# Flamingo block on one core: routing spread over ScalarE and GpSimd, and the turn of the maxima moved ahead of a score group

## The chip, the cores and the metric

One NeuronCore of a Trainium2 chip runs the whole kernel. The metric is device time in microseconds (us) of one launch. TensorE multiplies matrices, VectorE, ScalarE and GpSimd (POOL in the profile) work element by element, and SyncE only issues transfers; the engines run their own instruction lists side by side and meet at semaphores.

## What is computed

The input is 8 batches of 256 tokens of width 128, with 64 context rows per batch. First attention, then a mixture of experts, each added to its input through a gate:

```
x = x + tanh(g_xattn) * attention(layernorm(x), ctx)     # 16 heads of 8, keys = 64 ctx rows + 256 tokens, causal
x = x + tanh(g_ffn)   * experts(layernorm(x))

# experts: T = 2048 tokens, E = 8 experts, top 2 of each token, H = 512
logits = xt @ Wg + bg
top_v, top_i = top_k(logits, 2)
label = one_hot(top_i).sum(1)
seq = cumsum(label, 0) * label            # running place of each token in each expert
valid = seq <= capacity                   # capacity = 320; later tokens are dropped
h = silu(disp @ W1) * (disp @ W2);  out = h @ W3
y = sum over the two choices of softmax(top_v) * out[place]
```

## The kernel before

**Stages.** Up to about 34 us all queries, keys and values are made and stacked. Then a loop of ticks handles 16 units (a unit is half the heads, four pairs, of one batch); two units make a batch. Behind it (from about 223 us) the experts run one after the other: transfers bring each expert's 320 rows, TensorE and ScalarE and VectorE compute, and GpSimd adds the answers into the output with indirect transfers, three for each expert, one expert after the other.

**The order in the loop** is written out by hand: each tick has 16 slots (`SL`), and each step of a unit or batch has a place `AT_...` counted from that unit's own tick. Every engine walks through the same ticks and slots and issues its own steps in them, so the order on an engine is that of the slots, and within a slot that of its code (on VectorE the maxima come first). Nothing but semaphores ties an engine's slot to another's. For batches `b >= LATE` (the last two) some steps have places of their own (`LATE_...`). A step of a batch is counted from its second unit.

**One unit.** In tick U-2 TensorE makes the scores of four pairs p (`scores`, slots 0, 4, 8, 12) and VectorE takes their maxima (`maxima`, L835 and L836, slots 2, 6, 10, 14). In tick U-1 TensorE turns the maxima into a row (`maxima_t`, slot 4), ScalarE copies it (L689, slot 5), and SyncE's queue moves it beside the queries. In tick U the transposed scores are made (`scores_t`, L1100), together with the scores of unit U+2, ScalarE takes exponentials (L696), and GpSimd masks them (L577, L580). In tick U+1 come the products with the values (`values`, L1120, slots 5, 7, 9, 11, 13) and ScalarE's copy of them (L707, slot 15). In tick U+2 they are turned (`turn_values`, L1153), inverted and normalised (L841, L851).

**One batch** then goes on: attention turned (L1161), projected (L1170), added to x (L867, `x1_done`), statistics, rstd on GpSimd (L588), normalised tokens (`tokens_out`, L881), tokens turned (L1179), copied by ScalarE (L717, and L718 for the second copy of the row), logits (L1185), then routing: `top_two` on VectorE in eight steps (top values, indices, one-hot, labels, running count), `positions` on TensorE (running place by products with a triangle and with ones), `destinations` in five steps (weights, place, overflow, row number), and `send_rows`, four indirect transfers by GpSimd (L598) into a DRAM table `slots_dram`, cleared before in four transfers (L570). A row is 128 token values, the token number, and the weight.

**Shared memory.** The eight PSUM banks are shared by time: bank 6 holds the value products and the turned maxima, bank 7 the turned values, the logits, the positions and, in its other half, the projected tokens. Many waits of TensorE guard these: `values` waits for ScalarE's copy of the row (`mrow_done`), `turn_tokens` for the normalised attention of the next unit (`att_done`), `turn_values` for the positions to have been read, and `positions` for `x1_done` of the next batch when `b < LATE`. `keep_active` issues filler products (L1058) on TensorE where it would have little to do.

## Time and profile before

| | |
|---|---|
| three runs | 308.89, 305.91, 308.52 us; median 308.52 |
| the profiled execution | 304.91 us, of which 303.1 us is the span of the trace |
| mean granted TensorE clock | 0.905 of 2.4 GHz |
| busy: TensorE, VectorE, GpSimd, ScalarE | 238.4, 174.1, 152.9, 132.0 us |
| chain that ended last, by engine | TensorE 34%, VectorE 14%, issue 14%, transfers 13%, GpSimd 13%, ScalarE 5% |
| loop of ticks | from about 34 to 200 us |
| expert stage | from about 223 us to the end |

The columns of a timeline row are start and duration in us, the engine, the line of the kernel, the instruction, the tile written and the tiles read, shapes, and how many were merged; in brackets stands how long the engine sat idle before and what released it. The profile was taken of one execution, so its durations add up to that one.

### The profile page before, as it was taken

To read this page: it belongs to the slowest core of one execution; us is meant where nothing else is said; L and a number is where in the kernel's file an instruction comes from. 1 tells how busy PE (TensorE), PEld (TensorE's weight loads), DVE (VectorE), ACT (ScalarE), POOL (GpSimd) and SP (SyncE) were. 2 spreads that over 40 slices of the span, in tenths; PEclk is the share of its full clock that TensorE was granted. 3 is DMA by queue.
4 is the path that set the end of the run, shared out by engine and by line. 5 is a ranking of instruction groups with operands and counts; after the bars stand their busy time and mean duration, and the time that the engine had idled before them with its cause. 6 is when DMAs were issued, how large, how long until landed. Compare 5 with 4: busy or idle time off the path is not lost.

```text
span 303.1 us, 6031 instructions
## 1 busy us (share of the span) xinstructions
PE 238.4 (79%) x2179; PEld 140.7 (46%) x2179; DVE 174.1 (57%) x532; ACT 132.0 (44%) x294; POOL 152.9 (50%) x213
## 2 busy tenths in 40 slices
PE   1767784888988777897997789885979999999800
PEld 0555322355554444454554444342346666666600
DVE  6479691758889899877758963544102333333400
ACT  6256501757665566655546666312013333333200
POOL 3699820445352763817417548355500555655661
PEclk9999966979999999977569999997889999999985
DMA  7131365464533226561010001001054455553220
GB/s 199 38 84 47 67 118 85 76 119 99 118 57 58 54 51 94 106 190 43 16 37 13 16 18 40 0 16 43 4 122 125 118 120 125 126 127 57 22 22 5
DMA packets 28764, 21.79 MB, mean 72 GB/s; under 512 B 4105, under 2 KB 26051, under 8 KB 28736
## 3 DMA queue, kind: packets, MB, share of 16 engines
q1 hardware_dynamic: 21632, 15.74, 22.7%
q0 software_dynamic: 4608, 4.16, 7.9%
q10 hardware_dynamic: 2496, 1.52, 2.5%
q8 instruction: 17, 0.28, 0.4%
q14 instruction: 11, 0.09, 0.1%
HBM read 9.27 MB, written 5.82 MB: 50 GB/s over the span
## 4 chain that ended last, share of the span: by engine, by line
PE 34%; DVE 14%; issue 14%; DMA 13%; POOL 13%; ACT 5%; ACTq 2%; POOLq 1%; SPq 1%; another core or an unknown queue 0%; DVEq 0%
PE PS L1120 11%; DMA out<-kst 7%; PE PS L1100 6%; POOL out L633 5%; DMA qst<-mrow 4%; DVE rows L881 2%; PE PS L1083 2%; DVE mxb L836 2%; DVE mxb L835 2%; PE PS L1058 2%; PE PS L1170 2%; ACT pt L696 2%; POOL slots L598 2%; PE PS L1274 1%; PE PS L1276 1%
## 5 line engine op out<-in xcount | busy, mean ns | idle before, releaser
L696 ACT ACTIVATE pt<-PS 128x512 f32<-128x512 f32 x128 | 72.0, 596 | 41.5 <-PE PS L1100 38.8
L1100 PE MATMUL PS<-qst,kst 49*128 49x256 bf16 (+2 forms) x384 | 51.6, 250 | 8.1 <-DMA qst<-mrow 6.8
L633 POOL DMA_INDIRECT out<-kst x24 | 36.4, 1518 | 41.9 <-DVE kst L1004 19.0
L1120 PE MATMUL PS<-pt,vp 128*32 128x256 f32 (+2 forms) x768 | 47.8, 343 | 8.6 <-ACT mrow L689 7.5
L835 DVE TENSOR_REDUCE mxb<-PS 128x2 bf16<-128x384 f32 x64 | 35.5, 555 | 29.7 <-PE PS L1083 27.3
L836 DVE TENSOR_REDUCE mxb<-PS 128x2 bf16<-128x640 f32 x64 | 52.3, 817 | 0.0
L1100 PEld LDWEIGHTS PS<-qst,kst 49*128 49x128 bf16 x384 | 30.5, 100 | 31.5 <-issue 14.7
L991 DVE TENSOR_TENSOR kst<-PS,kst 128x320 f32<-128x320 f32 x32 | 15.7, 492 | 49.8 <-ACT kst L765 49.8
L598 POOL DMA_INDIRECT slots<-rows,dest x32 | 32.2, 1007 | 19.6 <-DVE dest L962 12.8
L577 POOL TENSOR_SCALAR_AFFINE_SELECT pt<-pt 128x512 f32<-128x512 f32 x32 | 21.5, 672 | 38.6 <-ACT pt L696 38.5
L1078 PE MATMUL PS<-kst,qst 48*128 48x320 bf16 x128 | 33.4, 335 | 0.0
L1075 PE MATMUL PS<-kst,qst 48*128 48x192 bf16 x128 | 30.1, 269 | 1.9 <-DVE work L805 1.4
L1083 PE MATMUL PS<-kmask,qmask 64*128 64x256 bf16 x128 | 31.1, 302 | 0.0
L1058 PE MATMUL PS<-ones 128*128 128x512 bf16 x90 | 29.1, 432 | 0.8 <-POOL pace L621 0.7
L1120 PEld LDWEIGHTS PS<-pt,vp 128*32 128x32 f32 x768 | 16.1, 113 | 22.0 <-issue 13.6
L765 ACT ACTIVATE kst<-PS 128x320 f32<-128x320 f32 x32 | 14.0, 437 | 26.9 <-PE PS L1276 26.9
L1274 PE MATMUL PS<-kst,kp 128*128 128x320 f32 x64 | 24.0, 458 | 0.6 <-ACT kst L746 0.6
L1276 PE MATMUL PS<-kst,kp 128*128 128x320 f32 x64 | 23.5, 450 | 0.0
L580 POOL TENSOR_SCALAR_AFFINE_SELECT pt<-pt 128x512 f32<-128x512 f32 x32 | 20.3, 634 | 0.0
L585 POOL TENSOR_SCALAR veps<-mv 128x2 f32<-128x2 f32 x8 | 1.5, 192 | 34.6 <-DVE mv L876 34.5
L1285 PE MATMUL PS<-kst,kp 128*128 128x320 f32 x56 | 16.7, 442 | 0.2
L1019 PE MATMUL PS<-ident,pt 128*128 128x128 f32 x20 | 5.0, 353 | 13.1 <-DVE pt L792 8.6
(129 smaller groups left out, 382.5 us busy)
## 6 DMA issues: line engine op xcount, KB each, us to landing
kp<-in_w SPq DMA_DIRECT2D x24, 256.0 KB, 2.9
kst<-kp SPq DMA_DIRECT2D x30, 80.0 KB
qst<-qp SPq DMA_DIRECT2D x36, 64.0 KB
slots<-blank POOLq DMA_DIRECT2D x4, 325.0 KB, 4.5
kst<-slots SPq DMA_DIRECT2D x8, 130.0 KB, 2.4
out<-xs SPq DMA_DIRECT2D x4, 256.0 KB
kst<-kp SPq DMA_DIRECT2D x14, 40.0 KB
xs<-in_x SPq DMA_DIRECT2D x2, 256.0 KB, 4.6
```

The lines of the kernel that those rows point to most:

```text
L598: nc.gpsimd.indirect_dma_start(out=slots_dram, out_offset=bass.IndirectOffsetOnAxis(ap=dest[:, b % 2, 2 * t + k:2 * t + k + 1], axis=0), i ...
L633: nc.gpsimd.indirect_dma_start(out=tokens, out_offset=bass.IndirectOffsetOnAxis(ap=ex[0:n, e, s, D:D + 1].bitcast(u32), axis=0), in_=yr[0: ...
L696: nc.scalar.activation(pt[:, U % 2, h, :], PS[:, 4 + h % 2, :], ACT.Exp, scale=SCALE).then_inc(exp_done, 1)
L835: nc.vector.tensor_reduce(mxb[:, U % 2, 0, :, p], PS[:, a:a + 2, 0:192], axis=AX.X, op=ALU.max)
L836: nc.vector.tensor_reduce(mxb[:, U % 2, 1, :, p], PS[:, a:a + 2, 192:512], axis=AX.X, op=ALU.max).then_inc(max_done, 1)
L1058: nc.tensor.matmul(PS[:, bank, :], ones[:, :], bass.AP(tensor=ov.tensor, offset=ov.offset, ap=[ov.ap[0], [0, 4], [1, 128]]), start=True, s ...
L1075: nc.tensor.matmul(bank[:, 0:192], queries_of(r, gp)[:, g0 + p, i, 0:128], keys_of(r, gp)[:, g0 + p, i, 0:192], start=True, stop=False)
L1078: nc.tensor.matmul(bank[:, 192:512], queries_of(r, gp)[:, g0 + p, i, 128:256], keys_of(r, gp)[:, g0 + p, i, :], start=False, stop=False)
L1083: c = nc.tensor.matmul(bass.AP(tensor=dst.tensor, offset=dst.offset, ap=[dst.ap[0], [320, 2], [1, 128]]), qmask[h, :], bass.AP(tensor=mk.t ...
L1100: c = nc.tensor.matmul(PS[:, 4 + par, c0:c1], keys_of(r, gp)[:, g0 + p, i, k0:k0 + 128], queries_of(r, gp)[:, g0 + p, i, q0:N], start=True ...
L1120: c = nc.tensor.matmul(O[VW * j:VW * j + VW, q0:N], vblock(b, chunk, g0 + j, par), pt[:, V % 2, 2 * j + par, c0:c1], start=(chunk == 0 and ...
L1274: nc.tensor.matmul(PS[:, 2 + n % 2, 0:CAP], w1s[:, e % 2, 128 * c:128 * c + 128], xT[:, e % 2, :], start=True, stop=True)
```

## The change

- **Order.** Most steps of a batch move by two or three slots; `turn_values` from slot 1 to 4, its inverse and product from 3 and 4 to 5 and 6, the residual add from 12 to 14, positions from 13 to 15. `maxima_t` comes ahead of the scores of p = 1 instead of behind the whole group. The late batches keep the common places for `top_two`, and their positions and destinations move back by six slots or more.
- **Tokens.** ScalarE writes both copies of the normalised tokens (`Identity` with scale rstd and bias -mean*rstd), GpSimd makes that bias; VectorE's `tokens_out` and ScalarE's copy L718 go.
- **Routing.** The one-hot is compared from the index as it is; the labels and the running count go. `positions` adds, by products with a matrix that has only its last row set (`lastrow`, fp32), a base of E values that is the last positions plus the expert's offset, so that what comes out is the row number itself. The table has 2048 rows for each expert (`places`), so no overflow test is needed; each expert reads its first 320. The destination is the largest of the masked positions.
- **Weights.** The exponential of the difference is taken by ScalarE in one operation per half; sum, inverse (a power of -1) and product go to GpSimd.
- **Normalising** is one operation instead of two, with the halves of a batch laid side by side, for which the output weights are loaded in four transfers instead of one. The table is cleared in eight transfers of half the size instead of four.

```diff
-    SLOTS = E * CAP
+    SLOTS = E * T
...
@@ -281,32 +278,32 @@
...
-        AT_OT = 2 * SL + 1
-        AT_INV = 2 * SL + 3
-        AT_NORM = 2 * SL + 4
-        AT_ATTT = 2 * SL + 6
-        AT_ATTC = 2 * SL + 8
-        AT_PROJ = 2 * SL + 10
-        AT_X1 = 2 * SL + 12
-        AT_STAT = (2 * SL + 13, 2 * SL + 15)
-        AT_RSTD = 2 * SL + 15
-        AT_TOK = 3 * SL + 2
-        AT_H2T = 3 * SL + 6
-        AT_H2C = 3 * SL + 8
-        AT_LG = 3 * SL + 10
...
-        AT_TOP = (3 * SL + 12, 3 * SL + 13, 3 * SL + 15, 4 * SL, 4 * SL + 1, 4 * SL + 3, 4 * SL + 5, 4 * SL + 6)
...
-        AT_E01 = 4 * SL + 4
-        AT_POS = 4 * SL + 13
-        AT_DEST = (4 * SL + 8, 4 * SL + 15, 5 * SL, 5 * SL + 1, 5 * SL + 2)
+        AT_OT = 2 * SL + 4
+        AT_INV = 2 * SL + 5
+        AT_NORM = 2 * SL + 6
+        AT_ATTT = 2 * SL + 8
+        AT_ATTC = 2 * SL + 10
+        AT_PROJ = 2 * SL + 12
+        AT_X1 = 2 * SL + 14
+        AT_STAT = (2 * SL + 15, 3 * SL + 1)
+        AT_RSTD = 3 * SL + 1
+        AT_TOK = 3 * SL + 6
+        AT_H2T = 3 * SL + 8
+        AT_H2C = 3 * SL + 10
+        AT_LG = 3 * SL + 12
+        AT_TOP = (3 * SL + 14, 3 * SL + 15, 4 * SL + 1, 4 * SL + 3)
+        AT_E01 = 4 * SL + 2
+        AT_WTS = 4 * SL + 6
+        AT_POS = 4 * SL + 15
+        AT_DEST = (5 * SL + 1, 5 * SL + 2)
         AT_SENT = (5 * SL + 4, 5 * SL + 6, 5 * SL + 12, 5 * SL + 20)
...
         LATE = B - 2
-        LATE_TOP = tuple(3 * SL + 12 + i // 2 for i in range(8))
-        LATE_E01 = 3 * SL + 14
-        LATE_POS = 3 * SL + 15
-        LATE_DEST = (3 * SL + 15, 4 * SL, 4 * SL + 1, 4 * SL + 1, 4 * SL + 2)
-        LATE_SENT = ((4 * SL + 3, 4 * SL + 4, 4 * SL + 20, 4 * SL + 21), (4 * SL + 3, 4 * SL + 4, 4 * SL + 5, 4 * SL + 6))
+        LATE_POS = 4 * SL + 5
+        LATE_DEST = (4 * SL + 7, 4 * SL + 8)
+        LATE_SENT = ((4 * SL + 9, 4 * SL + 10, 4 * SL + 20, 4 * SL + 21),
+                     (4 * SL + 9, 4 * SL + 10, 4 * SL + 11, 4 * SL + 12))
 
...
-                         (wos, wout), (bb, bout.partition_broadcast(128))):
+                         (bb, bout.partition_broadcast(128))):
                 sp.dma_start(s[:, :], w).then_inc(small_in, 16)
+            for m in range(UP):
+                sp.dma_start(wos[4 * HD * m:4 * HD * m + 4 * HD, :],
+                             wout.rearrange("(v m c) d -> m v c d", v=2, m=UP)[m]).then_inc(small_in, 16)
...
-            def clear_slots(n):
-                if n == 0:
+            def clear_slots(e):
+                if e == 0:
                     pool.wait_ge(consts, N_CONSTS)
-                nc.gpsimd.dma_start(slots_dram.rearrange("(p n) c -> p n c", p=128)[:, CLEAR * n:CLEAR * n + CLEAR, :],
-                                    blank[:, :, :]).then_inc(dram_zero, 16)
+                nc.gpsimd.dma_start(places[e * T:e * T + CAP, :].rearrange("(p n) c -> p n c", n=CLEAR),
...
@@ -587,16 +595,31 @@
                 pool.wait_ge(eps_added, len(GROUPS) + b + 1)
                 nc.gpsimd.tensor_tensor(rstd2[:, b % 2, :], veps2[:, b % 2, :], half[:, 0:2], ALU.pow
                                         ).then_inc(rstd_ready, 1)
+                pool.wait_ge(rstd_ready, len(GROUPS) + 2 * b + 1)
+                for t in range(2):
+                    c = nc.gpsimd.tensor_scalar(shift2[:, b % 2, t:t + 1], mv2[:, b % 2, t, 0:1],
+                                                rstd2[:, b % 2, t:t + 1], -1.0, ALU.mult, ALU.mult)
+                c.then_inc(rstd_ready, 1)
+
+            def weights(b):
+                pool.wait_ge(e01_done, b + 1)
+                nc.gpsimd.tensor_scalar(s01[:, :], e01[:, :], 1.0, 1.0, ALU.mult, ALU.add).then_inc(wts_done, 1)
+                pool.wait_ge(wts_done, S_WTS * b + 1)
+                nc.gpsimd.tensor_tensor(rows[:, b, 0, :, D + 1], s01[:, :], invert2[:, :], ALU.pow).then_inc(wts_done, 1)
+                pool.wait_ge(wts_done, S_WTS * b + 2)
+                nc.gpsimd.tensor_tensor(rows[:, b, 1, :, D + 1], e01[:, :], rows[:, b, 0, :, D + 1], ALU.mult
+                                        ).then_inc(wts_done, 1)
 
             def send_rows(b, n):
                 k, t = n // 2, n % 2
                 if n == 0:
                     if b == 0:
-                        pool.wait_ge(dram_zero, 16 * (SLOTS // 128 // CLEAR))
+                        pool.wait_ge(dram_zero, 16 * E)
                     pool.wait_ge(dest_ready, b + 1)
-                    pool.wait_ge(row1_done, b + 1)
+                    pool.wait_ge(h2_ready, b + 1)
+                    pool.wait_ge(wts_done, S_WTS * (b + 1))
                 nc.gpsimd.indirect_dma_start(
-                    out=slots_dram, out_offset=bass.IndirectOffsetOnAxis(
+                    out=places, out_offset=bass.IndirectOffsetOnAxis(
                         ap=dest[:, b % 2, 2 * t + k:2 * t + k + 1], axis=0),
                     in_=rows[:, b, k, t, :], in_offset=None,
                     bounds_check=SLOTS - 1, oob_is_err=False).then_inc(sent[b % 2], 16)
...
+
+            def tokens_out(b):
+                act.wait_ge(rstd_ready, len(GROUPS) + 2 * b + 2)
+                for i in range(2):
+                    xv = xs[:, 2 * b + i, :]
+                    c = nc.scalar.activation(rows[:, b, :, i, 0:D],
+                                             bass.AP(tensor=xv.tensor, offset=xv.offset, ap=[xv.ap[0], [0, TOPK], [1, D]]),
+                                             ACT.Identity, scale=rstd2[:, b % 2, i:i + 1],
+                                             bias=shift2[:, b % 2, i:i + 1])
+                c.then_inc(h2_ready, 1)
+
+            def second_exponentials(b):
+                act.wait_ge(top_ready, b + 1)
+                if b >= 1:
+                    act.wait_ge(wts_done, S_WTS * b)
+                for t in range(2):
+                    c = nc.scalar.activation(e01[:, t:t + 1], top[:, t, 0:1], ACT.Exp, scale=-1.0, bias=top[:, t, 1:2])
+                c.then_inc(e01_done, 1)
...
-            def tokens_out(b):
-                dve.wait_ge(rstd_ready, len(GROUPS) + b + 1)
-                for i in range(2):
-                    c = nc.vector.tensor_scalar(rows[:, b, 0, i, 0:D], xs[:, 2 * b + i, :], mv2[:, b % 2, i, 0:1],
-                                                rstd2[:, b % 2, i:i + 1], ALU.subtract, ALU.mult)
-                c.then_inc(h2_ready, 1)
-
...
@@ -890,77 +925,47 @@
                     nc.vector.tensor_tensor(lg[:, :, :], LOGITS, bg2[:, :, :], ALU.add).then_inc(route, 1)
                 if step == 1:
...
+                    if b >= 1:
+                        dve.wait_ge(e01_done, b)
                     for t in range(2):
                         c = nc.vector.max(top[:, t, :], lg[:, t, :])
-                    c.then_inc(route, 1)
+                    c.then_inc(top_ready, 1)
                 if step == 2:
-                    dve.wait_ge(route, r + 2)
+                    dve.wait_ge(top_ready, b + 1)
...
-                    nc.vector.tensor_tensor(d01[:, :], top[:, :, 1], top[:, :, 0], ALU.subtract).then_inc(d01_ready, 1)
                 if step == 3:
-                    dve.wait_ge(route, r + 3)
-                    nc.vector.tensor_copy(idxf[:, :].rearrange("p (t k) -> p t k", t=2), topi[:, :, 0:TOPK]
-                                          ).then_inc(route, 1)
...
-                                            ALU.is_equal).then_inc(route, 1)
-                if step == 5:
...
-                    nc.vector.tensor_tensor(lab[:, b % 2, :, :], ov[:, :, 0, :], ov[:, :, 1, :], ALU.add
-                                            ).then_inc(lab_ready, 1)
...
-                    nc.vector.tensor_tensor(run1[:, :], run[:, b % 2, :], lab[:, b % 2, 0, :], ALU.add
-                                            ).then_inc(route, 1)
-                if step == 7:
-                    dve.wait_ge(route, r + 6)
+                    dve.wait_ge(route, r + 2)
                     if b >= 1:
                         dve.wait_ge(pos_ready, b)
-                    nc.vector.tensor_tensor(run[:, (b + 1) % 2, :], run1[:, :], lab[:, b % 2, 1, :], ALU.add
-                                            ).then_inc(route, 1)
+                    iv = topi[:, :, :]
+                    nc.vector.tensor_tensor(oh[:, :, :].rearrange("p (t k) e -> p t k e", k=TOPK),
+                                            iotak[:, :, :].rearrange("p (t k) e -> p t k e", k=TOPK),
+                                            bass.AP(tensor=iv.tensor, offset=iv.offset,
+                                                    ap=[iv.ap[0], [8, 2], [1, TOPK], [0, E]]),
+                                            ALU.is_equal).then_inc(oh_ready, 1)
...
                 if step == 0:
...
-                    nc.vector.reciprocal(rows[:, b, 0, :, D + 1], s01[:, :]).then_inc(wts_done, 1)
+                    dve.wait_ge(oh_ready, b + 1)
                     dve.wait_ge(pos_ready, b + 1)
                     pv = positions_at(b)
                     nc.vector.tensor_tensor(ohp[:, :, :].rearrange("p (t k) e -> p t k e", k=TOPK),
                                             bass.AP(tensor=pv.tensor, offset=pv.offset,
                                                     ap=[pv.ap[0], [E, 2], [0, TOPK], [1, E]]),
                                             oh[:, :, :].rearrange("p (t k) e -> p t k e", k=TOPK),
-                                            ALU.mult).then_inc(wts_done, 1)
-                if step == 2:
-                    dve.wait_ge(wts_done, wr + 3)
-                    nc.vector.tensor_tensor(rows[:, b, 1, :, D + 1], rows[:, b, 0, :, D + 1], e01[:, :], ALU.mult)
...
-                    nc.vector.scalar_tensor_tensor(slotf[:, :], idxf[:, :], float(CAP), posk[:, :], ALU.mult, ALU.add
...
+                                            ALU.mult).then_inc(picked, 1)
+                    nc.vector.tensor_copy(base[:, (b + 1) % 2, :], pv[:, 1, :]).then_inc(base_ready, 1)
+                if step == 1:
+                    dve.wait_ge(picked, b + 1)
                     if b >= 2:
                         dve.wait_ge(sent[b % 2], 16 * 4 * (b // 2))
-                    nc.vector.scalar_tensor_tensor(dest[:, b % 2, :], slotf[:, :], -1.0, over[:, :], ALU.add, ALU.add
-                                                   ).then_inc(dest_ready, 1)
+                    nc.vector.tensor_reduce(dest[:, b % 2, :], ohp[:, :, :], axis=AX.X, op=ALU.max
+                                            ).then_inc(dest_ready, 1)
...
                 if V % 2 == 0 and V >= 4:
-                    pe.wait_ge(wts_done, S_WTS * (V // 2 - 2) + 3)
+                    pe.wait_ge(base_ready, V // 2 - 1)
...
@@ -1190,22 +1195,23 @@
 
                 if b == 0:
                     pe.wait_ge(consts, N_CONSTS)
-                pe.wait_ge(lab_ready, b + 1)
-                pe.wait_ge(route, S_ROUTE * b)
+                pe.wait_ge(oh_ready, b + 1)
+                if b >= 1:
+                    pe.wait_ge(base_ready, b)
 
                 if b < LATE:
                     pe.wait_ge(x1_done, b + 2)
-                elif b > LATE:
-                    pe.wait_ge(wts_done, S_WTS * (b - 1) + 3)
-                else:
+                elif b == LATE:
                     pe.wait_ge(max_done, UP * UNITS)
                 pos = positions_at(b)
-                cur, rn = lab[:, b % 2, :, :], run[:, b % 2, :]
-                nc.tensor.matmul(pos[:, 0, :], tri[:, :], cur[:, 0, :], start=True, stop=False)
-                nc.tensor.matmul(pos[:, 0, :], ones[:, :], rn, start=False, stop=True)
-                nc.tensor.matmul(pos[:, 1, :], tri[:, :], cur[:, 1, :], start=True, stop=False)
-                nc.tensor.matmul(pos[:, 1, :], ones[:, :], cur[:, 0, :], start=False, stop=False)
-                nc.tensor.matmul(pos[:, 1, :], ones[:, :], rn, start=False, stop=True).then_inc(pos_ready, 1)
+                before = base[:, b % 2, :]
+                for t in range(2):
+                    nc.tensor.matmul(pos[:, t, :], lastrow[:, :], before, start=True, stop=False)
+                    for i in range(2 * t):
+                        nc.tensor.matmul(pos[:, t, :], ones[:, :], oh[:, i, :], start=False, stop=False)
+                    nc.tensor.matmul(pos[:, t, :], tri[:, :], oh[:, 2 * t, :], start=False, stop=False)
+                    c = nc.tensor.matmul(pos[:, t, :], tri[:, :], oh[:, 2 * t + 1, :], start=False, stop=True)
+                c.then_inc(pos_ready, 1)
...
@@ -1217,6 +1223,8 @@
                     for p in range(UP):
                         if (U := due(tick, slot, AT_S2 + 4 * p)) in EVERY:
                             scores_t(U, p, 0)
+                        if p == 1 and (U := due(tick, slot, AT_MT)) in EVERY:
+                            maxima_t(U)
                         if (U := due(tick, slot, AT_S1 + 4 * p)) in EVERY:
                             scores(U, p)
...
@@ -1231,8 +1239,6 @@
                         if tick == UNITS - 2 and slot == 0:
                             pe.wait_ge(max_done, UP * UNITS)
                         keep_active(1, 2)
-                    if (U := due(tick, slot, AT_MT)) in EVERY:
-                        maxima_t(U)
```

## Rows read from the trace of the kernel before

**Rows 1.** Stretch, span; busy PE, PEld, DVE, ACT, POOL; clock, DMA, GB/s.

```profile
98.00:178.00 80.00, 67.22 (x889) 39.23 (x887) 64.35 (x210) 46.58 (x100) 41.49 (x59) 0.87 0.27 59
```

**Rows 2.** Waits, whole span: waiter <- releaser: total us, times, longest.

```profile
PE PS L1120 <- ACT mrow L689: 7.5, 12, 0.9
...
PE PS L1179 <- DVE work L851: 5.1, 7, 1.2
...
PE PS L1161 <- DVE work L851: 1.2, 2, 0.8
```

**Rows 3.** TensorE's timeline, 112 to 130 us: start, duration, instruction [idle before].

```profile
113.99 0.71 PE L1170 MATMUL PS<-wos,work 128*128 128x128 f32 x4
...
115.10 0.28 PE L1100 MATMUL PS<-qst,kst 49*128 49x256 bf16 x1
...
115.80 0.43 PE L1120 MATMUL PS<-pt,vp 128*32 128x64 f32 x16
116.16 0.18 PE L1204 MATMUL PS<-lab,tri 128*128 128x8 bf16 x1
...
116.37 0.28 PE L1100 MATMUL PS<-qst,kst 49*128 49x256 bf16 x1
...
119.45 0.64 PE L1120 MATMUL PS<-pt,vp 128*32 128x256 f32 x8 [0.54 <-ACT mrow L689]
...
122.83 0.61 PE L1185 MATMUL PS<-wgs,work 128*128 128x8 f32 x4
...
129.02 0.88 PE L1120 MATMUL PS<-pt,vp 128*32 128x256 f32 x8 [0.85 <-ACT mrow L689]
```

**Rows 4.** Groups by line: busy us, mean ns | idle before.

```profile
L881 DVE TENSOR_SCALAR rows<-xs,mv,rstd 128x128 f32<-128x128 f32 x16 | 7.6, 517 | 2.4 <-POOL rstd L588 2.4
...
L901 DVE TENSOR_TENSOR d<-top 128x2 f32<-128x2 f32 x8 | 3.6, 446 | 0.0
...
L588 POOL TENSOR_TENSOR rstd<-veps,half 128x2 f32<-128x2 f32 x8 | 5.8, 720 | 0.7
...
L718 ACT COPY rows<-rows 128x256 f32<-128x256 f32 x8 | 3.3, 408 | 0.0
...
L570 POOL DMA_DIRECT2D slots<-blank x4 | 2.4, 593 | 0.0
...
L585 POOL TENSOR_SCALAR veps<-mv 128x2 f32<-128x2 f32 x8 | 1.5, 192 | 34.6 <-DVE mv L876 34.5
```

**Rows 5.** ScalarE's timeline, two ticks: waits before the maxima row is out.

```profile
118.36 0.60 ACT L696 ACTIVATE pt<-PS 128x512 f32<-128x512 f32 x1 [0.42 <-PE PS L1100]
...
128.51 0.36 ACT L689 CAST mrow<-PS 8x256 bf16<-8x256 f32 x1 [0.41 <-PE PS L1135]
```

**Rows 6.** TensorE's timeline while the loop of ticks fills.

```profile
58.09 0.28 PE L1100 MATMUL PS<-qst,kst 49*128 49x256 bf16 x1 [0.41 <-DMA qst<-mrow]
```

**Rows 7.** VectorE's timeline around slots 12 to 15 of the same odd tick.

```profile
114.80 0.47 DVE L867 SCALAR_TENSOR_TENSOR xs<-PS,tgx,xs 128x256 f32<-128x256 f32 x1
...
115.87 0.56 DVE L835 TENSOR_REDUCE mxb<-PS 128x2 bf16<-128x384 f32 x1
...
117.07 0.24 DVE L876 BATCH_NORM_AGGREGATE mv<-stats 128x2 f32<-128x6 f32 x2
```

**Rows 8.** SyncE's queue (SPq) at the start: issue start us, us, line.

```profile
7.33 1.49 SPq L403 DMA_DIRECT2D kst<-minus  x2
11.21 4.00 SPq L352 DMA_DIRECT2D qst<-qp  x6
```

**Rows 9.** VectorE's timeline for the last batch: masked positions and destinations.

```profile
212.26 0.17 DVE L944 TENSOR_TENSOR ohp<-PS,oh 128x32 f32<-128x32 f32 x1
...
213.02 0.17 DVE L962 SCALAR_TENSOR_TENSOR dest<-slotf,over 128x4 uint32<-128x4 f32 x1
```

**Rows 10.** Two stretches of two ticks each; columns as in rows 1.

```profile
137.77:160.72 22.95, 20.75 (x220) 11.60 (x217) 15.38 (x51) 11.58 (x25) 9.97 (x15) 0.63 0.08 24
160.72:178.58 17.86, 14.82 (x212) 8.48 (x209) 15.36 (x50) 11.27 (x25) 10.23 (x15) 1.00 0.04 13
```

124 lines of the change are left out of this document (54 added, 70 removed).

## The prediction

> **What bounds the kernel now.** I read the busy times by stretch first. From 98 to 178 us, where every batch is scored and routed, TensorE is busy 67.2 of 80 us and VectorE 64.4 [rows 1]; the expert stage behind it the change does not enter, except by the place of its rows. So the span is set by how TensorE's hand-written slots run, and a change on another engine counts only through a wait of TensorE or through the routing of the last batch, which nothing covers.
>
> The list of waits says which. TensorE stood 7.5 us for the row of maxima that ScalarE copies (L689), 5.1 us at the turn of the tokens (L1179) for VectorE's normalised attention, and 1.2 us for the same at L1161 [rows 2]. Two ticks of TensorE's timeline give the lengths. Call G12 and G0 the groups of scores at slots 12 and 0. In the odd tick G12 starts at 115.10, the last value products at 115.80, the positions at 116.16, G0 at 116.37, the next first value products at 119.45 (wait 0.54). In the following tick those products start at 129.02, after a wait of 0.85 [rows 3].
>
> **Work taken off VectorE.** Eleven small operations per batch go, or leave for other engines; the two costliest are the tokens (L881, 7.6 us in all) and the difference of the top two (L901, 3.6) [rows 4]. VectorE is off the end-setting path in between: this is worth only the waits it caused. The turn of the tokens waited for L851, which stood in VectorE's queue behind L881. The tokens are ScalarE's now, and normalising comes at slot 6 with the turn at slot 8, a score group and two value steps later. I take the 5.1 us as gone, and 0.8 of the 1.2 at L1161 (its worst case; the rest is in the last batch, where the order is a plain chain): **-5.9**. Ends: 0, if something else is late at the same slot, and -6.3.
>
> **Maxima turned in front.** `maxima_t` moves ahead of the scores of p = 1. Both already wait for the same maxima, so no wait is added to the scores behind it. What ScalarE must do before copying the row is not changed: the exponentials of the same half. In one tick ScalarE sat 0.41 us for the turned maxima, in the other 0.42 us for the scores in front, which now start right after G0 since the turn of the values moved from slot 1 to slot 4 [rows 5]. I take 0.42 for 12 ticks: **-5.0**. Ends 0 and -7.5. Filling the loop, the row of the second unit leaves earlier, by the scores and filler products it now stands in front of, and 0.41 us of wait on its transfer goes [rows 6]: **-0.4**.
>
> **The new waits.** Positions moved from slot 13 to 15, the residual add (`x1`, L867) from 12 to 14, and at slot 14 VectorE's loop takes the maxima of p = 3 before it. TensorE's `positions` waits for `x1_done` of the next batch in six of eight batches. From G12 at 115.10 VectorE's maxima began at 115.87 and it was free at 117.07; the add took 0.47 [rows 3, 7]. That is 1.97 + 0.48 + about 0.1 for the signal = 2.55 us after G12. TensorE gets there after 0.70 for the group, 0.71 for the projection (now at slot 12) and 0.36 for the last value step, 1.77 us [rows 3]. It stands 0.8 us, with the next group queued behind it and ScalarE and VectorE fed by that: 6 x 0.8 = **+4.8**. Ends: 0, if the queues are so late that both meet, and 1.2 more each if VectorE is a pair behind, +12.
>
> **Positions themselves.** Five bf16 products took 0.21 us (116.16 to 116.37). Now there are eight, two of them fp32 with fp32 weights. No such pair is in the trace; the nearest is the logits, two fp32 products of eight columns in 0.61 us [rows 3]. So 0.6 more per batch, six in the loop: **+3.6**; ends 0.1 and 0.7 each.
>
> **What I cost at nothing.** ScalarE's tokens (two passes in place of one copy of 0.41 us, L718 [rows 4]) run behind the exponentials while TensorE does two value steps; ScalarE is busy 47 of 80 us [rows 1]. Uncovered, they would be some 0.4 us a batch. The Trainium skill speaks against this move: "ScalarE: Activation LUTs" (Rules for kernel authors) wants such arithmetic on VectorE, and its cost formula (What ACT_TABLE_LOAD costs) gives an estimated 1.1 us for the two passes, 0.7 more than the copy; by it the last batch would be 0.3 us worse than below. GpSimd's weights (three operations, one a power like the rstd's 0.72 us, the others like veps's 0.19) and two products for the shift, some 1.5 us a batch [rows 4], lie where it is busy 41 of 80 us. The clearing in eight transfers instead of four adds four issues of 0.59 us [rows 4] on its queue in the first four ticks, where it waits for exponentials; three more loads on SyncE's queue, at most 0.75 us each like the two issues that ended at 8.82, fall in its gap up to 11.21 [rows 8].
>
> **The end.** For the last batch, everything is serial. GpSimd's shift adds about 0.5 (two products of 0.19 and a signal [rows 4]), ScalarE's tokens 0.1, the positions 0.6. Gone are the difference, the cast, the label add (about 0.5), and from the masked positions at 212.26 to the destinations at 213.02 the 0.76 us becomes 0.35, with one reduction behind one product and a copy [rows 9]. GpSimd's weights run while TensorE does positions. **+0.2**, between -1 and +1.5.
>
> **Sum.** -5.9 - 5.0 - 0.4 + 4.8 + 3.6 + 0.2 = **-2.7 us**. The profiled execution took 304.91 us (span 303.1, the rest around it), so it would take 302.2; it stands 3.6 below the median of the three runs, 308.52, and on that the same change gives **305.8 us**. About 1%, 3.1 us, is what a measurement of this kernel can tell from no change.
>
> **Rivals.**
> *The positions' wait decides (slower).* Same mechanism as above, but the gains at the maxima row do not come, because ScalarE's chain (values copy, two exponentials, weights' exponential, a third exponential, row) binds at the same instant, and only the token wait is recovered: -5.9 + 8.4 + 0.2 = +2.7; with VectorE a further 0.4 us late at the add, 6 x 0.4 more, +5.1, so 311 to 314. It decides once TensorE's stand at positions passes 0.8 us. For it: VectorE is busy 80% there [rows 1]. Against: less work on VectorE. Chance 0.20.
>
> *VectorE was the real pace (clearly faster).* If its delays also cause part of the remaining waits, the whole 7.5 goes and the add finds an empty queue: another -2.5 - 3, so 298 to 302. For it: L901 averages 446 ns for two numbers a partition, so it is being held up [rows 4]. The Trainium skill, "GPSIMD Engine Reference" (Key points), says that GpSimd shares its SBUF interfaces with VectorE and contends with VectorE's instructions of two SBUF inputs; that rule also speaks against the weights on GpSimd, whose hold would fall on whatever VectorE does then. Against: VectorE idles at TensorE's groups each tick. Chance 0.15.
>
> *The clock moves instead.* From 137.8 to 160.7 the granted clock was 0.63, largely its lower level, 1.2 GHz, and two ticks took 22.95 us; the next two at 1.00, 2.4 GHz, took 17.86 [rows 10]. TensorE was busy 90% of the slow stretch, so the row does not show idleness as the cause. One stretch more or less is 5.1 us, either way: 300 or 311. Chance 0.08 each way, inside the others' ranges.
>
> *It does not reach the time (no change).* Waits shift one slot on and the sum is zero, 307.5 to 310. Chance 0.12, beside what it shares with the forecast.
>
> **Numbers.** Forecast, 303 to 307.5, 0.37; positions' wait 0.20; clearly faster 0.15; clock 0.16; no change 0.12. Under 305.4: half the forecast, the fast rival, one clock case: 0.42. Over 311.6: most of the slow rival and a little of the clock: 0.20. Between: 0.38. The range 299 to 312.5 leaves out about 0.05 below and 0.14 above.
>
> **What would show it.** Right: L1179's wait on L851 gone; L1120's wait on L689 below 4 us; TensorE standing 0.6 to 1 us before the positions in six ticks, released by L867; eight position products in about 0.8 us; 17.2 to 17.6 us from batch to batch at full clock. Wrong: no wait at positions, or one above 1.5 us; value products still waiting 0.5 us or more for the row in every tick; the tokens' turn waiting for ScalarE; table loads on ScalarE beyond the two.

## The result and the profile after

The changed kernel took 295.52 us (median of 4 runs, 293.94 to 295.81), the kernel before 308.19 (4 runs, 305.91 to 308.89): ratio 0.9591, 95% interval [0.953, 0.9652], faster. The forecast, 305.8 in a range from 299.0 to 312.5, was wrong: the time lies 3.5 us under its lower end. Unchanged copies run again gave 298.10 and 298.08 for after, 306.28 and 310.07 for before. By the medians of the three sessions that held both kernels the gain is 12.7, 8.7 and 9.0 us. Each ratio here and below compares only the runs within 1.5% of the fastest of their own kernel in the session, and since before scatters most, these runs alone give less: ratios of 0.9591, 0.9827 and 0.9897, or about 12.6, 5.3 and 3.1 us. Only the first of the three is clearly faster at a mark of 2%; the sign is the same in all, the size is not settled. An interval also understates what separates two copies: b_again came out at 1.0209 [1.0133, 1.0285] against its own original in the same session.

The profiled execution of after took 295.71 us (span 293.9, clock 0.906); before took 304.91. TensorE's waits over the whole span, waiter and releaser, total us, times, longest, the answer to [rows 2]:

```profile
PE PS L1103 <- DMA qst<-mrow: 7.3, 3, 6.2
...
PE PS L1103 <- ACT pt L722: 5.1, 15, 0.4
...
PE PS L1209 <- DVE xs L909: 4.4, 6, 0.8
PE PS L1184 <- ACT rows L749: 4.4, 2, 4.1
PE PS L1078 <- DVE mxb L879: 1.6, 5, 0.4
...
PE PS L1138 <- DVE mxb L879: 0.4, 1, 0.4
PE PS L1123 <- ACT mrow L715: 0.2, 1, 0.2
```

The wait for the row of maxima fell from 7.5 to 0.2; those at the tokens' turn for VectorE (5.1) and at the attention's (1.2) are gone. New are the positions' (4.4 over six, released by the residual add) and one that the prediction did not have: scores waiting for ScalarE's exponentials, 5.1 where before had 0.6. Before had waits that I left out of the sum too, at the turn of the values (L1153) and for GpSimd's selects:

```profile
PE PS L1153 <- ACT work L707: 2.0, 3, 0.9
PE PS L1153 <- DVE ohp L944: 1.8, 4, 0.5
...
PE PS L1120 <- POOL pt L577: 0.6, 1, 0.6
PE PS L1120 <- POOL pt L580: 0.5, 1, 0.5
```

A second profile of the same kernel (b_same) has:

```profile
PE PS L1120 <- ACT mrow L689: 7.0, 12, 0.8
...
PE PS L1179 <- DVE work L851: 5.1, 7, 1.2
...
PE PS L1161 <- DVE work L851: 3.8, 5, 0.8
...
PE PS L1153 <- DVE ohp L944: 1.8, 4, 0.5
```

In after the turn of the values waits for neither inside the loop. In b_same the 2.0 is absent and the attention's turn waits 3.8 instead of 1.2; b_again is like the first profile (2.5 and 1.2). So these two rows trade places between executions of one kernel. The positions in after, on TensorE's timeline (start, duration, idle before), beside [rows 3]:

```profile
112.10 0.71 PE L1175 MATMUL PS<-wos,work 128*128 128x128 f32 x4
112.74 0.43 PE L1123 MATMUL PS<-pt,vp 128*32 128x64 f32 x16
113.99 0.36 PE L1209 MATMUL PS<-base,lastrow 128*128 128x8 f32 x2 [0.82 <-DVE xs L909]
...
114.26 0.37 PE L1209 MATMUL PS<-base,lastrow 128*128 128x8 f32 x2
...
114.66 0.28 PE L1103 MATMUL PS<-qst,kst 49*128 49x256 bf16 x1
```

From 113.99 to 114.66 the eight products take 0.67 us (0.21 before), behind a stand of 0.82. The groups that answer to [rows 4] (busy us, mean ns | idle before):

```profile
L749 ACT ACTIVATE rows<-xs,shift,rstd 128x256 f32<-128x256 f32 x16 | 8.7, 591 | 7.5 <-POOL shift L600 7.5
L608 POOL TENSOR_TENSOR rows<-s,invert 128x2 f32<-128x2 f32 x8 | 5.8, 720 | 0.7
...
L600 POOL TENSOR_SCALAR shift<-mv,rstd 128x1 f32<-128x1 f32 x16 | 4.0, 264 | 0.8
L760 ACT ACTIVATE e<-top 128x1 f32<-128x1 f32 x16 | 3.8, 292 | 1.6 <-DVE top L931 1.6
```

Where the time went is read from three stretches, cut at the first value product of units 3 and 13, which the change does not move. Columns as in [rows 1]: stretch, length, busy TensorE, its loads, VectorE, ScalarE, GpSimd, granted clock, DMA. Before:

```profile
0.00:83.81 83.81, 58.76 (x548) 36.00 (x548) 57.85 (x139) 43.53 (x99) 44.85 (x90) 0.90 0.45 95
83.81:179.40 95.59, 80.19 (x1077) 46.64 (x1078) 78.26 (x250) 55.73 (x121) 48.52 (x70) 0.89 0.27 58
179.40:303.04 123.64, 99.45 (x554) 58.04 (x554) 38.01 (x147) 32.71 (x76) 59.56 (x54) 0.92 0.31 67
```

After:

```profile
0.00:81.66 81.66, 57.86 (x548) 37.12 (x548) 56.77 (x134) 43.52 (x99) 47.98 (x99) 0.92 0.45 96
81.66:172.38 90.72, 82.42 (x1104) 51.63 (x1103) 64.17 (x178) 60.15 (x133) 57.71 (x98) 0.88 0.32 65
172.38:293.77 121.39, 96.94 (x570) 60.16 (x569) 32.60 (x107) 34.60 (x80) 62.34 (x66) 0.92 0.33 74
```

The loop's ten ticks went from 95.59 to 90.72 us although the clock was no better (0.89 and 0.88). Length times clock is a rough loop length at full clock (rough, since waits for other engines don't shrink with TensorE's clock): 85.1 before, 79.8 after. I call it the product below.

### The profile page after: what moved, and what is told of

It is laid out like the page before. It is cut to its first block, busy times and chain, and to the rows that moved or that the text cites. A ratio compares the mean times of both kernels' runs of the same rounds, so it can differ in the third digit from the quotient of the medians.

```text
span 293.9 us, 6082 instructions
## 1 busy us (share of the span) xinstructions
PE 237.2 (81%) x2219; PEld 148.9 (51%) x2219; DVE 153.5 (52%) x419; ACT 138.3 (47%) x310; POOL 168.0 (57%) x261
## 4 chain that ended last, share of the span: by engine, by line
PE 37%; POOL 16%; DMA 14%; issue 13%; ACT 7%; DVE 5%; SPq 3%; ACTq 3%; POOLq 1%; DVEq 0%
PE PS L1123 10%; PE PS L1103 8%; DMA out<-kst 8%; POOL out L659 5%; DMA qst<-mrow 4%; ACT pt L722 3%; POOL places L621 3%; PE PS L1061 2%; PE PS L1086 2%; PE PS L1156 2%; PE PS L1078 2%; PE PS L1081 2%; ACTq L358 1%; DVE mxb L879 1%; PE PS L1209 1%
## 5 line engine op out<-in xcount | busy, mean ns | idle before, releaser
L1103 PE MATMUL PS<-qst,kst 49*128 49x192 bf16 (+2 forms) x384 | 51.2, 250 | 12.6 <-DMA qst<-mrow 7.3
L1123 PE MATMUL PS<-pt,vp 128*32 128x256 f32 (+2 forms) x768 | 42.6, 343 | 0.3 <-ACT mrow L715 0.2
L621 POOL DMA_INDIRECT places<-rows,dest x32 | 32.2, 1006 | 13.3 <-issue 7.1
L1081 PE MATMUL PS<-kst,qst 48*128 48x320 bf16 x128 | 29.2, 322 | 0.0
L1078 PE MATMUL PS<-kst,qst 48*128 48x192 bf16 x128 | 26.5, 264 | 3.0 <-DVE mxb L879 1.6
L1061 PE MATMUL PS<-ones 128*128 128x512 bf16 x90 | 27.9, 426 | 0.0
L1086 PE MATMUL PS<-kmask,qmask 64*128 64x256 bf16 x128 | 26.9, 290 | 0.0
L1123 PEld LDWEIGHTS PS<-pt,vp 128*32 128x32 f32 x768 | 19.2, 116 | 13.2 <-issue 9.1
L1280 PE MATMUL PS<-kst,kp 128*128 128x320 f32 x64 | 23.4, 447 | 0.6 <-ACT kst L790 0.6
L1282 PE MATMUL PS<-kst,kp 128*128 128x320 f32 x64 | 22.4, 432 | 0.0
L1291 PE MATMUL PS<-kst,kp 128*128 128x320 f32 x56 | 16.7, 442 | 0.2
L1282 PEld LDWEIGHTS PS<-kst,kp 128*128 128x128 f32 x64 | 12.2, 190 | 5.1
```

The lines of the kernel that those rows point to most:

```text
L621: nc.gpsimd.indirect_dma_start(out=places, out_offset=bass.IndirectOffsetOnAxis(ap=dest[:, b % 2, 2 * t + k:2 * t + k + 1], axis=0), in_=r ...
L1061: nc.tensor.matmul(PS[:, bank, :], ones[:, :], bass.AP(tensor=ov.tensor, offset=ov.offset, ap=[ov.ap[0], [0, 4], [1, 128]]), start=True, s ...
L1078: nc.tensor.matmul(bank[:, 0:192], queries_of(r, gp)[:, g0 + p, i, 0:128], keys_of(r, gp)[:, g0 + p, i, 0:192], start=True, stop=False)
L1081: nc.tensor.matmul(bank[:, 192:512], queries_of(r, gp)[:, g0 + p, i, 128:256], keys_of(r, gp)[:, g0 + p, i, :], start=False, stop=False)
L1086: c = nc.tensor.matmul(bass.AP(tensor=dst.tensor, offset=dst.offset, ap=[dst.ap[0], [320, 2], [1, 128]]), qmask[h, :], bass.AP(tensor=mk.t ...
L1103: c = nc.tensor.matmul(PS[:, 4 + par, c0:c1], keys_of(r, gp)[:, g0 + p, i, k0:k0 + 128], queries_of(r, gp)[:, g0 + p, i, q0:N], start=True ...
```

## The experiments

Six to ten runs each; kernels b_ start from before, a_ from after; medians and ranges are of all runs, the products of one profile each. Four profiles are of executions well above their kernel's median: a_best 297.05 us, a_pos1_again 296.19, b_otslot 304.03, b_slotsfront 294.46. The record classes every ratio in this table as unclear at 2%, also those whose interval lies below 0.98. So small differences between rows prove nothing alone.

| kernel | median us (range) | ratio to before, interval | loop us, clock, product |
|---|---|---|---|
| b_same | 306.28 (304.68 to 310.90) | 1.0073 [0.9991, 1.0155] | 97.78, 0.86, 84.1 |
| b_again | 310.07 (304.54 to 314.24) | 1.0209 [1.0133, 1.0285] | 101.48, 0.85, 86.3 |
| b_front | 304.75 (302.54 to 306.61) | 1.0048 [0.9963, 1.0133] | 98.81, 0.84, 83.0 |
| b_otslot | 299.79 (296.73 to 304.03) | 0.9856 [0.9762, 0.995] | 95.23, 0.87, 82.8 |
| b_tok | 298.71 (293.06 to 301.99) | 0.9722 [0.9568, 0.9876] | 89.90, 0.92, 82.7 |
| b_slots | 292.56 (290.65 to 295.97) | 0.9635 [0.9553, 0.9718] | 85.65, 0.91, 77.9 |
| b_slots_again | 295.93 (294.89 to 298.71) | 0.9866 [0.9794, 0.9938] | 88.85, 0.91, 80.9 |
| b_slotsfront | 291.40 (286.78 to 294.46) | 0.952 [0.9388, 0.9652] | 87.33, 0.92, 80.3 |
| b_slotspos1 | 295.83 (292.22 to 301.52) | 0.9711 [0.959, 0.9833] | 87.20, 0.96, 83.7 |
| a_same | 298.10 (297.10 to 298.90) | 0.9827 [0.9753, 0.9901] | 91.09, 0.88, 80.2 |
| a_again | 298.08 (297.26 to 299.04) | 0.9897 [0.9853, 0.9942] | 90.22, 0.88, 79.4 |
| a_tokv | 298.36 (296.65 to 299.02) | 0.9822 [0.9758, 0.9886] | 91.55, 0.88, 80.6 |
| a_back | 297.51 (296.08 to 299.39) | 0.9829 [0.9744, 0.9913] | 87.94, 0.90, 79.1 |
| a_late | 296.04 (295.00 to 298.98) | 0.9772 [0.9674, 0.9871] | 89.53, 0.89, 79.7 |
| a_ot1 | 294.50 (293.55 to 297.30) | 0.9706 [0.9626, 0.9786] | 86.29, 0.92, 79.4 |
| a_pos1 | 292.04 (291.50 to 293.54) | 0.964 [0.9564, 0.9716] | 83.87, 0.94, 78.8 |
| a_pos1_again | 292.55 (288.57 to 296.19) | 0.9561 [0.9453, 0.9669] | 87.36, 0.90, 78.6 |
| a_best | 292.70 (291.80 to 297.05) | 0.9743 [0.9696, 0.9789] | 89.07, 0.89, 79.3 |

**Is a stretch at the lower clock part of the result?** b_same, b_again, a_same and a_again are copies, no edit.

> The kernel before, unchanged. Asked here: whether the long stretch at the lower clock (17 us at about 150 us in the profiled execution of before, none as long in the one of after) belongs to the kernel or to that execution. Theory 'waits' (the gain of 12.7 us between the medians is TensorE's waits that went, about 9, and the rest is chance of the stretch): time 306 to 309, the low stretches lie elsewhere in this profile, and where they don't, the intervals between the maxima's turns agree with those of before within 0.3 us. Theory 'clock' (the kernel before falls into the lower clock in the middle of the loop because of the order of its work): the long stretch shows again between 137 and 170 us.

> Before, unchanged, a third profile. Theory 'places set the clock': a low-clock stretch of 13 us or more between 80 and 180 us of the span, and 20 us or more of low clock there. Rival 'chance': no stretch above 10.3 us.

> The kernel after, unchanged: a second and third look at its clock. Theory 'clock' (the new places keep TensorE from the long low-clock stretch): 294 to 297, no low stretch longer than 10.3 us between 80 and 180 us, and 14 to 21 us of low clock in that part where before had 20 to 27. Rival 'chance': a stretch of 13 us or more shows in the loop, as in before and b_front.

> After, unchanged, a third profile, in the same call as b_slots_again and a_best so that they can be compared: 295 to 298.5; no low-clock stretch above 10.3 us between 80 and 180 us by the theory 'places set the clock', one by 'chance'.

b_same showed a stretch as long as that of [rows 10], at the same place; b_again showed none, but several short ones, and was the slowest of the three. Stretches of b_same, then of b_again:

```profile
120.00:143.00 23.00, 18.05 (x279) 11.05 (x276) 21.31 (x70) 14.42 (x32) 12.52 (x19) 0.98 0.51 119
143.50:160.00 16.50, 15.96 (x150) 8.62 (x143) 9.15 (x29) 7.47 (x16) 6.92 (x10) 0.52 0.11 32
```

```profile
97.00:103.00 6.00, 6.00 (x73) 3.47 (x65) 3.02 (x9) 2.13 (x4) 0.00 (x0) 0.55 0.45 70
103.50:116.50 13.00, 8.99 (x134) 5.50 (x133) 11.61 (x41) 8.11 (x19) 9.51 (x13) 0.98 0.25 52
117.50:123.50 6.00, 6.00 (x53) 3.07 (x54) 2.88 (x8) 1.69 (x4) 0.52 (x1) 0.55 0.47 81
```

TensorE was busy 78% in the 23 us before the fall in b_same, 97% in it, and 100% in the two of b_again. So the long stretch is not a fixed property of the order. What is left is a level: the three loops of before stood at 0.89, 0.86 and 0.85, those of after at 0.88 each. Loop less product, a rough price of the lower clock, is 10.5, 13.7 and 15.2 us before, 10.9, 10.9 and 10.8 after: 2.3 us less on average. Whether the change causes that, three profiles a side don't settle. But the level does go with the kernel: the three profiles with the new places on before's operations (b_slots twice, b_slotsfront) stood at 0.91, 0.91 and 0.92, the four with the old places at 0.84 to 0.89. Why is open.

The record also has the granted clock of each whole run. Over the 73 runs of before and its copies the time falls by some 2.2 us for each 0.01 of clock, with 1.6 us of scatter about that line. Against this line, each run at its own clock, the three sets of after lie 9.1, 7.5 and 8.6 us lower; b_slots 9.4 and 7.6; b_slotsfront 10.2; b_tok 7.6; b_otslot 1.7; b_front 1.9; a_back 7.6; a_pos1 8.9 and 10.0; a_ot1 12.3. These are estimates, good to 1 us at best, from a correlation: after's own 20 runs lie along a flatter line, 0.7 us for each 0.01.

**The maxima's turn alone.** b_front adds it to before, a_back takes it from after.

```diff
                     for p in range(UP):
...
+                        if p == 1 and (U := due(tick, slot, AT_MT)) in EVERY:
+                            maxima_t(U)
...
-                    if (U := due(tick, slot, AT_MT)) in EVERY:
-                        maxima_t(U)
```

> Before, with the one edit that the two maxima of a unit are turned in front of the scores of p = 1. Theory 'waits': the value products' wait for the row of maxima (7.5 us) falls to below 3 us and the time by 4 to 7 us, to 301 to 304. Rival 'VectorE' (the row was late because the copy of the values before it on ScalarE was late in every second tick, held by what VectorE and GpSimd do then): the wait stays above 5 us in those ticks and the time falls by less than 3 us, 305 to 308.

> After, with the two maxima turned behind the scores of p = 1 again. Theory 'places': in b_slots, where they stand behind, the row's wait was 1.8 us and the time no worse than with them in front, so within 2 us of after, 294 to 297.5; the row's wait 1 to 2 us. Rival 'front' (my prediction's term, 5 us): 299 to 301.

Waits of TensorE in b_front, then in a_back:

```profile
PE PS L1179 <- DVE work L851: 5.8, 7, 1.2
...
PE PS L1120 <- ACT mrow L689: 3.3, 11, 0.8
...
PE PS L1153 <- DVE ohp L944: 1.6, 4, 0.5
```

```profile
PE PS L1103 <- ACT pt L722: 4.9, 14, 0.4
PE PS L1209 <- DVE xs L909: 4.4, 6, 0.8
...
PE PS L1123 <- ACT mrow L715: 1.7, 7, 0.5
```

The row's wait fell by 4.2 us in b_front, and the time by 2.1 at most (304.75 beside 306.81 for before in the same session, ratio 1.0048), which is within the scatter. In a_back the wait came back by 1.5 and the time stood (297.51 beside 298.10 for a_same in the same session). b_front's product is 2.2 below before's, a_back's no higher than after's. Neither kernel did what the prediction's 5 us would give, and b_front's wait ended between its two expectations (below 3, above 5).

**The new places alone.** b_slots gives before the places of after, but not to the slot: its tokens come one slot earlier (3 * SL + 5), and its late batches are routed two slots behind before's, four ahead of after's. b_otslot moves the values' turn (and the two turns behind it), b_tok the tokens' side; b_slotsfront adds the maxima in front to b_slots.

```diff
-        AT_OT = 2 * SL + 1
-        AT_INV = 2 * SL + 3
-        AT_NORM = 2 * SL + 4
-        AT_ATTT = 2 * SL + 6
+        AT_OT = 2 * SL + 4
+        AT_INV = 2 * SL + 5
+        AT_NORM = 2 * SL + 6
+        AT_ATTT = 2 * SL + 8
...
-        AT_H2T = 3 * SL + 6
-        AT_H2C = 3 * SL + 8
-        AT_LG = 3 * SL + 10
+        AT_H2T = 3 * SL + 8
+        AT_H2C = 3 * SL + 10
+        AT_LG = 3 * SL + 12
...
-        AT_POS = 4 * SL + 13
+        AT_POS = 4 * SL + 15
```

> Before, with only the new places of the work of a batch: the values turned at slot 4, normalised at 6, tokens turned at slot 8, positions at slot 15, and so on; the operations and their engines are as before. Theory 'waits': the waits at the turn of the values (3.8 us) and of the tokens (5.1) go, a wait of 0.8 us at six positions comes (+4.8): 2 to 5 us faster, 303 to 306. Rival 'VectorE': with VectorE's eleven small operations still there the waits only move, and the time is within 2 us of before, 306 to 309.

> Before, with the maxima turned in front and the new places, operations and engines as before. Theory 'waits': this is the whole of the gain in the order of work; the time is that of after less the price of the longer positions (about 3 us) plus what VectorE's small operations cost, 294 to 298. Rival 'VectorE': the operations that left VectorE bring the gain, so this is 301 or above.

> Before, with fewer new places: the values turned at slot 4 instead of 1 (invert 5, normalise 6), and because of it the attention turned at 8 (copied at 9) and the tokens at 8 (copied at 9); projection, residual add, statistics, positions and destinations stay. Theory 'values' turn' (the place of this turn alone makes the row of maxima late and costs the waits at three turns, 3.8 + 5.1 + 1.2 us, and the long low-clock stretch): 291 to 295, no wait at the positions, the wait for the row below 2.5 us. Rival 'all places': the gain needs the shift of the rest too, 298 to 304.

> Before, with the new places of the tokens' side only (tokens turned at 8, copied at 10, logits at 12, routing behind, positions at 15); values' and attention's turns stay. Theory 'values' turn': the wait at the tokens' turn (5.1 us) goes, the one for the row (7.5) and at the values' turn (3.8) stay, the positions wait little (the residual add is still at 12): 302 to 306. Rival 'token turn': the tokens' turn was what made the rest late, 291 to 296.

> The kernel before with only the new places, once more. Theory 'the rebuilt routing costs time' (eight position products in 0.69 us in place of five in 0.21, the shift and ScalarE's two passes at the end): 2 to 5 us below after in this call. Rival 'equal': within 1.5 us of after.

b_slots has the whole gain, with every operation still on its old engine and the maxima's turn in its old place: 292.56 and 295.93 us, 14.3 and 11.2 below before in the same sessions. b_slotsfront, with the maxima in front too, is no different within the scatter (291.40 beside 292.56). The waits of b_slots:

```profile
PE PS L1100 <- ACT pt L696: 5.4, 16, 0.4
...
PE PS L1204 <- DVE xs L867: 4.4, 6, 0.8
...
PE PS L1120 <- ACT mrow L689: 1.8, 8, 0.5
```

In the loop they are those of after, with 1.8 in place of 0.2 for the row. The two halves are worth 2.4 and 2.5 us in product, together some 5.8 (mean of b_slots' two profiles, 79.4, against 85.2). By medians they stand 7.5 (b_otslot) and 8.6 us (b_tok) below before's 307.28 in their session, and by the line of clock and time 1.7 and 7.6. The three measures disagree, so how the gain splits between the halves is open. b_otslot took the row's wait from 7.5 to 2.2 without touching the maxima's turn, but was slower than its theory said and still had the tokens' turn waiting:

```profile
PE PS L1100 <- ACT pt L696: 7.7, 13, 1.4
PE PS L1179 <- DVE work L851: 4.6, 6, 1.3
...
PE PS L1120 <- ACT mrow L689: 2.2, 6, 0.8
```

In b_tok the tokens' turn no longer waits for VectorE, and TensorE still waits for the row:

```profile
PE PS L1120 <- ACT mrow L689: 6.5, 12, 0.5
PE PS L1161 <- DVE work L851: 4.2, 4, 1.4
PE PS L1100 <- ACT pt L696: 3.2, 5, 1.3
```

Its 298.71 us missed both of its expectations (302 to 306, and 291 to 296). So most of the row's wait could stay (6.5 of 7.5) and the time still fall.

In the session with a_again, b_slots stood 2.15 us below it (295.93 and 298.08), the intervals overlapping: the engine moves and the longer positions together bring nothing that can be told apart from zero, or cost 2 us. The first theory of b_slots_again had said 2 to 5.

**Undoing single parts of after.** a_tokv gives the tokens back to VectorE. a_ot1 turns the values at slot 1 again (inverse 3, product 4). a_late lets VectorE make the tokens of the last batch only.

```diff
-        AT_OT = 2 * SL + 4
-        AT_INV = 2 * SL + 5
-        AT_NORM = 2 * SL + 6
+        AT_OT = 2 * SL + 1
+        AT_INV = 2 * SL + 3
+        AT_NORM = 2 * SL + 4
```

```diff
-            def tokens_out(b):
-                act.wait_ge(rstd_ready, len(GROUPS) + 2 * b + 2)
...
+                    c = nc.vector.tensor_scalar(rows[:, b, 0, i, 0:D], xs[:, 2 * b + i, :], mv2[:, b % 2, i, 0:1],
+                                                rstd2[:, b % 2, i:i + 1], ALU.subtract, ALU.mult)
```

> After, with the tokens normalised by VectorE again (and the second row copied by ScalarE), the rest as in after. Theory 'places' (the gain comes from the order, the moves off VectorE bring nothing): within 1.5 us of after (295.5), 294 to 297; the last batch is about 1 us shorter at the tokens. Rival 'VectorE' (tokens off VectorE bring the gain at the turn of the tokens): 299 to 302, with a wait of L1184-like turns for VectorE of 4 us or more.

> After, with the values turned at slot 1 again, in front of the second group of scores (inverted at 3, normalised at 4), all else as in after, the maxima's turn in front too. Theory 'place of the values' turn' (it stands between two groups of scores and waits for ScalarE's copy; what ScalarE and the row of maxima wait for is late by it): the wait for the row comes back to 3 us or more, and waits of 2 to 4 us at the values' turn; time 3 to 6 us above a_pos1_again plus its 5 to 6, so 300 to 304. Rival 'maxima in front' (the step of the prediction: 0.42 us a tick): the wait for the row stays below 1 us, time 297 to 299.

> After, with the tokens of the last batch alone normalised by VectorE (ScalarE copies its second row). Theory 'serial end' (nothing covers the shift on GpSimd and the pass on ScalarE there): the wait at the last turn of the tokens falls from 4.1 to 2.7 us, the end comes 1 to 1.6 us earlier, 293.5 to 295. Rival 'hidden': the rows are gathered no earlier, because another wait (positions for the mask, or the sends) ends at the same time: no change, 295.5.

a_tokv is the equal of after's copies (298.36, ratio 0.9822, against 298.10 and 0.9827 for a_same in another session). In a_late the last turn of the tokens waits 0.5 us, where it waits 2.8 in a_same, and its time is 2.1 us below a_same in the same session, with overlapping intervals: likely, not shown. a_ot1 was a miss for the theory that I had by then, that the values' turn between two score groups makes the row late:

```profile
PE PS L1209 <- DVE xs L909: 4.4, 6, 0.8
PE PS L1156 <- ACT work L733: 2.5, 1, 2.5
...
PE PS L1123 <- ACT mrow L715: 1.2, 6, 0.4
...
PE PS L1103 <- ACT pt L722: 1.1, 2, 0.8
```

The row waits 1.2 us, and the new wait for the exponentials is nearly gone, 5.1 to 1.1. So that wait comes from the values' turn having left its place in front of the group at slot 4. In after, slot 4 saves nothing that these runs show: a_ot1's 294.50 us is below all three medians of after, though no copy of after ran in its session, and its product (79.4) is the same as theirs.

**The stand at the positions.** a_pos1 puts the positions behind the next tick's first scores; a_best adds a_late to it; b_slotspos1 does it on b_slots.

```diff
-        AT_POS = 4 * SL + 15
-        AT_DEST = (5 * SL + 1, 5 * SL + 2)
+        AT_POS = 5 * SL + 1
+        AT_DEST = (5 * SL + 2, 5 * SL + 3)
```

> b_slots with the positions behind the scores of the next tick's slot 0 (slot 1 of the next tick), destinations one slot on. Theory 'queue' (TensorE stands 0.8 us at six positions because the residual add is late, with the next scores queued behind): the wait of 4.4 us goes, 3 to 4.5 us faster than b_slots (292.6), 288 to 290. Rival 'the pace is elsewhere' (ScalarE's exponentials or the clock bind as soon as TensorE is early): the waits for the exponentials grow by as much, 291 to 294.

> After, with the positions one slot later, behind the scores of the next tick's slot 0 (destinations one slot on). Theory 'every wait elsewhere' (as in b_slotspos1: the stand of 0.8 us at the positions goes and comes back at the turns of values and tokens): 294 to 298, no gain. Rival 'queue' (in after VectorE has no queue to hold those turns up): 290 to 292.5, 4.4 us of waits gone.

> a_pos1 once more, after with the positions behind the next scores: 291.5 to 293.5, as before, if its 6 us below after is its own; 296 to 298 if it was chance of the clock (its loop stood at 0.94 of full clock against 0.88 in after).

> After with the positions behind the next scores (as in a_pos1) and the last batch's tokens on VectorE (as in a_late): both gains add if they are what they seem, 4.4 to 6 us and 1 to 1.6 us below after, 289.5 to 292. Rival 'not additive': no better than a_pos1, 292.

Waits in b_slotspos1, then in a_pos1:

```profile
PE PS L1100 <- ACT pt L696: 5.0, 12, 1.0
...
PE PS L1179 <- DVE work L851: 3.5, 5, 1.1
PE PS L1161 <- DVE work L851: 3.2, 3, 2.2
PE PS L1153 <- DVE ohp L944: 3.0, 4, 0.8
```

```profile
PE PS L1103 <- ACT pt L722: 6.2, 14, 0.9
...
PE PS L1156 <- DVE base L962: 0.7, 4, 0.2
```

With VectorE's small operations still there, the 4.4 us came back at the three turns (2.2 in b_slots, 9.7 here); with them gone, only 1.1 + 0.7 did. a_pos1 was 6.06 us below a_same in its session, the intervals apart, and a_best 5.4 below a_again, the intervals apart: 292.0 to 292.7 us, below both kernels. The product is only about 1 us lower. Most of the rest goes with the clock: a_pos1's six runs had a mean whole-run clock of 0.921, a_same's 0.900, which along before's line is worth some 4.6 us (along after's flatter one, 1.5). Why that clock is higher is open. a_late's part does not add.

## Why the prediction was wrong

The step that failed is what the prediction did with the new places. It counted them as a cost alone (the positions' wait, +4.8) and gave the gain to two other edits: the maxima turned in front (-5.0) and the work taken off VectorE (-5.9). The runs show the reverse. The places without either edit (b_slots) stand 14.3 and 11.2 us below before, the maxima's turn alone (b_front) 2.1 within the scatter, and after without the maxima's turn (a_back) or with the tokens back on VectorE (a_tokv) is no slower than after. Of the signs that I gave for being right, the waits all came; the last did not: 79.8 us of product for five batches are about 16.0 a batch (17.0 before), not 17.2 to 17.6.

**Work taken off VectorE** (-5.9): the waits went, 6.3 us, but not for that reason. b_slots keeps the work on VectorE and loses most of them (5.1 to 1.1 at the tokens' turn), and a_tokv gives tokens back at no cost. The rule of the Trainium skill, "GPSIMD Engine Reference" (Key points), fits the row that I read it beside: L901's slowest, 1.06 us against 0.14 for the fastest, ran beside GpSimd's selects. Taking L901 away was not tried alone. The work off VectorE seems to pay only once the positions move: a_pos1's products are 78.8 and 78.6, b_slotspos1's 83.7, where VectorE's lateness is what the next turns meet. The ratios overlap (0.964 and 0.9711), so this is argued, not shown; which of the removed operations matters was not tried.

**Maxima turned in front** (-5.0, fill -0.4): the wait was sized well and its worth was not. It fell by 4.2 in b_front, close to my 5.0, and by 7.3 in after; it has two causes of which either removed takes most (b_front left 3.3, b_otslot 2.2, b_slots 1.8). Added alone it bought 2 us at most. Its own yield may lie in the lead: before unit 3's products, 81.66, 81.86 and 81.67 us in after against 83.81, 84.22 and 85.96 before, 2.9 less where I had 0.4; b_front shows 81.47 and a_back 84.72, but b_slotsfront 86.90, so it is not shown.

**The new waits** (+4.8): 4.4, as said: 0.82 in five batches and 0.3 in the sixth, released by the add. Left out was the group of scores at slot 4, in front of which nothing stands now that the values' turn has moved behind it: it waits for the exponentials, +4.5 (0.6 to 5.1), and the maxima's waits are up 1.3.

**Positions themselves** (+3.6): 0.46 x 6 = +2.8.

**Left out of the sum**: the values' turn, 3.8, and 1.1 of waits for GpSimd's selects (L577, L580), gone. With these rows: -6.3 - 7.3 - 4.9 + 4.5 + 1.3 + 4.4 + 2.8 = -5.5. My loop terms gave -2.5. These rows are of the whole span; the products, which give -5.3 for the profiled pair, are of ten ticks. Inside those ten ticks TensorE's waits fell from 15.1 to 8.0 us, and with five groups of positions at 0.46 that is -4.8, so waits explain the loop at full clock to within 0.5 us.

**What the error is made of.** The three profiled spans of before average 305.5 us, those of after 295.5. Of these 10.0 us the loop at full clock is 5.4 (forecast 2.5), the clock in the loop 2.3, which I had at 0.08 as a rival of its own and never beside the forecast, the lead 2.9 (forecast 0.4), and the end, which grew, takes back 0.5 (forecast 0.2). The first comparison's 12.7 is 2.7 more; the other two sessions gave 8.7 and 9.0, so I put that to the scatter, without a run that shows it.

**What I cost at nothing**: tokens on ScalarE took 1.09 us for the two passes; the formula of the Trainium skill, "ScalarE: Activation LUTs" (What ACT_TABLE_LOAD costs), gave an estimated 1.1, and the trace agrees. The page's advice to keep such work on VectorE made no difference here (a_tokv). At the end it shows: the last turn of the tokens waits 4.1 us, or 2.8 behind a wait of 1.9 at the last turn of the values (a_same and a_again), instead of 2.6. **The end** (+0.2): behind unit 13's products 121.39, 123.35 and 124.34 us against 123.64, 121.35 and 122.51, on average +0.5 within a scatter of 3.

**Rivals**: "VectorE was the real pace" named the right wait (all but 0.2 of the 7.5) and, with 298 to 302, came nearest to the copies' 298.1; but its reason was wrong, as b_slots shows, and the add found no empty queue. "The positions' wait decides" had the wait and not the missing gain.

## What to carry to other kernels

List every wait of the bounding engine in the loop, small ones too, before summing: four rows of 0.5 to 2 us, left out, came to 4.9 us, more than the forecast sum. Run a copy of the kernel before reading a small row: the 2.0 us of one of them was absent in b_same. Where two edits cut the same wait, neither's share is its own; only adding and removing each shows it. Price a new place by what it frees as well as by what it makes wait. A stand that stays after a change is worth a second placing (a_pos1).
